# Value products of a slot in two halves by queries, between the score products of the third and fourth head

## The reference

```
h   = layernorm(x) * (1 + ca) + sa                    # ca, sa, ga ... from silu(c) @ wmod, by batch
q, k, v = split(h @ w_qkv)                            # 16 heads of width 8
attn = softmax(q @ k.T / sqrt(128))                   # by head, 512 x 512
x   = x + ga * (concat(attn @ v) @ w_out)
h   = layernorm(x) * (1 + cb) + sb
x   = x + gb * moe(h)                                 # 8 experts of width 176, the best 2 of each token
```

## Time and profile before

| | us |
|---|---|
| median of 3 runs | 652.09 |
| lowest, highest | 651.35, 652.54 |
| the profiled execution's own time | 652.5 |
| its span, first to last instruction | 650.7 |

### The profile page before, as it was taken

How to read it: one execution, slowest core, us unless ns; L and a number is a source line. 1 busy time by engine, 2 the same in 40 slices (tenths; PEclk the granted TensorE clock), 3 DMA queues, 4 the chain that set the end, 5 groups by cost and what they waited for, 6 DMA issues and landing times.

```text
span 650.7 us, 10486 instructions
## 1 busy us (share of the span) xinstructions
PE 600.9 (92%) x3349; PEld 277.9 (43%) x3349; DVE 540.3 (83%) x1025; ACT 433.7 (67%) x823; POOL 300.0 (46%) x426
## 2 busy tenths in 40 slices
PE   4299999999999999999999999897999999999995
PEld 3112222332332322332332322235777777777773
DVE  3698898998998998998998998528788888888884
ACT  1206888788788888888888878774655555555552
POOL 4434205325315315415415212536576776776763
PEclk9757999999999999999999999899899999999998
DMA  7711803402503404404404401263245445444401
GB/s 187 177 65 37 240 3 76 157 19 69 165 19 91 143 20 93 139 21 100 133 19 101 142 9 48 67 191 99 97 133 149 135 136 152 135 136 148 136 24 33
DMA packets 49094, 65.77 MB, mean 101 GB/s; under 512 B 9544, under 2 KB 30544, under 8 KB 49040
## 3 DMA queue, kind: packets, MB, share of 16 engines
q1 hardware_dynamic: 46416, 64.32, 34.3%
q10 hardware_dynamic: 2624, 0.79, 0.6%
HBM read 47.26 MB, written 17.83 MB: 100 GB/s over the span
## 4 chain that ended last, share of the span: by engine, by line
PE 51%; DVE 19%; POOL 15%; issue 6%; ACT 5%; DMA 1%; SPq 1%; POOLq 0%; DVEq 0%; ACTq 0%
PE o_acc L1199 18%; PE s_row L1172 15%; POOL hid_lo L611 11%; DVE negmax L859 8%; DVE probs L1061 8%; PE s_col L1185 7%; ACT hid_hi L795 3%; POOL h_lo L617 2%; PE misc L1137 1%; PE misc L1153 1%; PE misc L1123 1%; PE misc L1120 1%; DVE probs L1051 1%; ACT probs L655 1%; SPq L295 1%
## 5 line engine op out<-in xcount | busy, mean ns | idle before, releaser
L859 DVE TENSOR_REDUCE negmax<-s_row 128x1 f32<-128x512 f32 x512 | 321.3, 682 | 36.9 <-PE s_row L1172 36.1
L655 ACT ACTIVATE probs<-s_col 128x512 f32<-128x512 f32 x512 | 273.3, 599 | 70.7 <-PE s_col L1185 68.5
L1172 PE MATMUL s_row<-k_stack,q_stack 64*128 64x512 bf16 x512 | 140.0, 402 | 21.8 <-DMA k_stack<-k_scr 11.2
L611 POOL TENSOR_TENSOR hid_lo<-probs,hid_hi 128x512 fp32r<-128x512 f32 x87 | 128.5, 1493 | 62.5 <-ACT hid_hi L795 62.5
L1199 PE MATMUL o_acc<-probs,v_aug 128*32 128x512 f32 x1024 | 137.2, 608 | 0.0
L1185 PE MATMUL s_col<-q_stack,k_stack 64*128 64x512 bf16 x512 | 127.5, 381 | 3.2 <-ACT probs L655 2.9
L795 ACT ACTIVATE hid_hi<-probs 128x512 fp32r<-128x512 f32 x88 | 55.6, 632 | 85.3 <-DVE probs L1061 85.3
L1172 PEld LDWEIGHTS s_row<-k_stack,q_stack 64*128 64x128 bf16 x512 | 35.3, 93 | 174.4 <-DVE negmax L859 131.9
L498 POOL CAST negmax_parts<-negmax 128x16 bf16<-128x16 f32 x32 | 6.3, 197 | 154.1 <-DVE negmax L859 154.1
L1061 DVE TENSOR_TENSOR probs<-probs,q_stack 128x512 f32<-128x512 f32 x56 | 61.9, 1106 | 15.4 <-POOL hid_lo L611 14.2
L1051 DVE TENSOR_TENSOR probs<-probs,s_col 128x512 f32<-128x512 f32 x88 | 59.6, 677 | 2.2 <-ACT probs L815 2.1
(11 more groups left out here) (144 smaller groups left out, 697.6 us busy)
## 6 DMA issues: line engine op xcount, KB each, us to landing
q_scr<-q_parts SPq DMA_DIRECT2D x48, 128.0 KB, 2.4
k_scr<-k_parts SPq DMA_DIRECT2D x48, 128.0 KB, 2.4
q_stack<-q_scr SPq DMA_DIRECT2D x8, 768.0 KB, 6.4
k_stack<-k_scr SPq DMA_DIRECT2D x8, 768.0 KB, 8.2
q_stack<-combT_scr SPq DMA_DIRECT2D x24, 256.0 KB, 3.5
k_stack<-combT_scr SPq DMA_DIRECT2D x16, 224.0 KB, 3.0
q_stack<-combT_scr SPq DMA_DIRECT2D x16, 192.0 KB, 2.8
q_stack<-combT_scr SPq DMA_DIRECT2D x16, 160.0 KB, 2.6
```

What stands on the lines that cost most here:

```text
L611: nc.gpsimd.tensor_tensor(hid_lo[k % HIDDEN][:], weighed[(par + k) % 2], hid_hi[k % HIDDEN][:], ALU.subtract).then_inc(s["hid_split"], 1)
L655: nc.scalar.activation(probs[t % 2][:, j, :], s_col[score_bank("col", u)][:], ACT.Exp, scale=INV_SCALE).then_inc(s["exp_done"], 1)
L859: nc.vector.tensor_reduce(negmax[n % 2][:, j, qc:qc + 1], s_row[score_bank("row", u)][:], AX.X, ALU.max, negate=True).then_inc(s["row_max" ...
L1172: nc.tensor.matmul(s_row[score_bank("row", u)][:], q_stack[par][at:at + KS, head // 2, P * qc:P * (qc + 1)], k_stack[par][at:at + KS, head ...
```

## The change

The change splits the value products of a slot into two halves by queries. Part 0 (queries 0 to 255) is issued right after the column scores of head 2, part 1 (queries 256 to 511) where all stood before. Part 0 takes the wait for the exponentials, and part 1 raises `pv_done`. In the four slots whose products open or close a sum in `o_acc` (0, 7, 8 and 15), part 0 is empty and part 1 makes them whole, as before; as slot t makes the products of slot t - 1, these are made in slots 1, 8, 9 and 0 of the loop. The other twelve slots of a batch (2 to 7 and 10 to 15 of the loop) are split.

```diff
-            def weigh(b, par, t):
+            def weigh(b, par, t, part):
                 n, kc = t // CH, t % CH
-                pe.wait_ge(s["exp_done"], UNITS * b + G * (t + 1))
                 m, i = n // SHARE, n % SHARE
                 first_of, last_of = i == 0 and kc == 0, i == SHARE - 1 and kc == CH - 1
+                whole = first_of or last_of
+                if whole and part == 0:
+                    return
+                if whole or part == 0:
+                    pe.wait_ge(s["exp_done"], UNITS * b + G * (t + 1))
                 if first_of and not (isinstance(b, int) and b == 0 and m == 0):
                     pe.wait_ge(s["o_saved"], NO * b + m)
                 values = v_aug[par][:].rearrange("p k h w -> p k (h w)")
+                half = N // 2
+                lo, hi = (0, N) if whole else (half * part, half * (part + 1))
                 for j in range(G):
                     at = VW * (G * n + j) + ROOM * (SHARE - 1 - i)
-                    last = nc.tensor.matmul(o_acc[VW * j:VW * (j + 1), :], values[:, kc, at:at + VW],
-                                            probs[t % 2][:, j, :], start=first_of, stop=last_of)
-                last.then_inc(s["pv_done"], 1)
+                    last = nc.tensor.matmul(o_acc[VW * j:VW * (j + 1), lo:hi], values[:, kc, at:at + VW],
+                                            probs[t % 2][:, j, lo:hi], start=first_of, stop=last_of)
+                if part == 1:
+                    last.then_inc(s["pv_done"], 1)
...
                 for t in range(SLOTS):
+                    def values(part):
+                        if t > 0:
+                            weigh(b, par, t - 1, part)
+                        elif not first:
+                            weigh(b - 1, 1 - par, SLOTS - 1, part)
...
                         for j in range(2 * half, 2 * half + 2):
                             scores(j)
                             col_scores(b, par, t, j)
+                            if j == 2:
+                                values(0)
                         turn((t, half))
-                    if t > 0:
-                        weigh(b, par, t - 1)
-                    elif not first:
-                        weigh(b - 1, 1 - par, SLOTS - 1)
+                    values(1)
                     turn((t, 2))
```

More of the change, by code:

```diff
@@ L1323, in block_body @@
                     if first and k == 0:
-                        weigh(B - 1, 1, SLOTS - 1)
+                        weigh(B - 1, 1, SLOTS - 1, 0)
+                        weigh(B - 1, 1, SLOTS - 1, 1)
                     if first:
```

## The result

The changed kernel takes 679.26 us (median of 4 runs, 676.8 to 689.97) where the kernel before took 652.32 us (4 runs). The ratio is 1.040, with an interval of 1.036 to 1.044: slower. The profiled execution took 677.85 us with a span of 676.0 us, 25.3 us more than the span before.

The account below looks back on a forecast made before the run. PE was taken to set most of a batch, a loop with DVE the slots without a task. Batches 1 to 6 +25.3 us, batch 0 +0.5, batch 7 +1.3: +27.1, forecast 679.2 us, range 666 to 690.

Parts of the forecast that it names:

- step 1: On PE, separating heads 2 and 3 turns 0.53 us into 0.53 + 0.53: +0.53 us wherever the pair ran beside itself.
- step 2: On PE, half of the value products takes 0.57 us, two halves 1.14, so +0.14 us.
- step 3: The 8 weight loads and 8 matmuls more per split slot on PE cost nothing.
- rival C: PE's instruction issue becomes the bound, about 717 us; weaker form, halves of 0.70 us, 696 us; together 15%.
- Rival A: On PE, changes of shape cost nothing extra and heads 2 and 3 overlap with the half between: 647 us, 5%.
- Rival B: Halves cost 0.50 us each, part of the broken pair hides behind waits in slots 4, 5, 14: about 666 us, 17%.
- Rival D: The halves are merged or the order on PE is not kept: 652 us, 1%.
- step 4: The wait for the exponentials moves in front of head 3's scores, but has passed by then: zero cost.
- step 5: In slots without a task, DVE's wait goes: 2.64 us in place of 2.70, set by PE.

## Why the prediction was right

**The broken pair (step 1)** was the number on which the forecast turned, and it held: a lone head takes 0.53 to 0.54 us between two shapes, in any of the three places where runs put it, and where pairs do not exist the split slot costs 0.25 us instead of 0.66.

**The half (step 2)** was put at 0.57 us and took 0.57. That the 0.14 us in it belong to the change of shape is now shown and not argued: two halves in a row take 1.00 us. The rule of the Trainium skill that changing the tiling mode drains the TensorE (TensorEngine Tiling (Array Packing), Key Properties) agrees with these runs: 0.14 us more for halves apart, nothing for halves in a row. The estimate from the fixed part of an isolated matmul (TensorE: Matmul & The Clock Gate, Single matmul latency), 0.33 us for two changes, was too high; the trace has 0.25.

**The instructions (step 3)** cost nothing, as the run with both halves at the end shows. That takes the strong form of rival C away, and the lone 0.57 its weak form. Rival A, no cost for changes of shape, fails on the 0.25 us and on the lone head's 0.54. Rival B wanted halves of 0.50 us and fails on the 0.57; of the slots in which it would hide a part, 4 and 5 cost what was forecast, and only slot 14 cost less. Rival D fails on the 1792 matmuls.

**The moved wait (step 4)** costs nothing that shows: in PE's list of waits no value product waits for ACT, in either trace.

**The gain in plain slots (step 5)** is there at its size, 2.64 us. That DVE's wait can be taken out of these slots is shown by the version with part 0 between the pairs in them alone. How much of the 0.06 us a batch keeps is less sure: with part 0 in the given place, and only there, the whole kernel cannot be told from before.

By slots, forecast and measured from one start to the next: slot 2 3.79 and 3.80; slots 3 and 4 3.32 and 3.33; 5 3.49 and 3.51; 6 3.82 and 3.83; 7 2.64 and 2.64; 10 3.32 and 3.34; 11 3.72 and 3.73; 12 2.81 and 2.81; 13 2.64 and 2.64; 15 3.32 and 3.28. Three sizes were off.

- Slot 14 had 0.25 us for a wait of PE for DVE. It is 3.33 us with no such wait; the row scores of head 1 start together with those of head 0 at 249.43. This is 1.5 us over six batches, and more than all of the difference between 25.3 and 24.2 us; against it the unsplit slots 8 and 9 took 6.24 us in place of 6.17. I had also taken one middle batch for all six; batches 1 and 6 took 48.39 us before and not 48.10.
- Batch 0 was +0.77 instead of +0.5.
- Batch 7 was +0.73 instead of +1.3. Here the clock took part. These stretches lie at the same place of both traces (x1T, the value products behind it and the router; the second is 1 us longer), before and after, with the granted clock in the third column from the end:

```profile
418.00:423.00 5.00, 4.07 (x20) 1.35 (x19) 1.61 (x2) 2.30 (x5) 2.03 (x2) 0.66 0.23 69
```

```profile
444.00:450.00 6.00, 5.07 (x51) 2.33 (x43) 1.99 (x4) 3.97 (x9) 3.42 (x3) 1.00 0.34 109
```

Before, the value products of slot 10 ran at half clock (1.91 us for what takes 1.06), after they did not. PE waited 0.93 us for POOL just ahead of them in both traces, so that pause alone does not decide it. The version with both halves at the end had a granted clock of 1.00 in all of batch 7 and took 43.91 us there:

```profile
391.63:435.54 43.91, 38.25 (x350) 14.84 (x347) 25.82 (x64) 36.38 (x70) 18.35 (x26) 1.00 0.34 96
```

Against it the changed kernel is 1.96 us longer, more than the 1.3 that I had said.

The sum of the profiled executions is thus 25.3 us against my 27.1. The median, 679.26 against 679.2, agrees better than the steps do, and that is chance: it counts the execution of 689.97 us, and without it the median is 677.85.

## What to carry to other kernels

Before something is put between two matmuls, look whether they run beside each other on different rows: two lines of the timeline that start together, with a time no longer than one alone, are one piece of work, and cutting it costs a whole second piece. A finer interleaving pays each change of shape on PE (0.10 to 0.14 us here), so do it only in those slots where PE has a pause, and put the cut at a place where a pair ends. Against some 652.5 us before, part 0 between the pairs took 648.2 us in slots with a pause alone and 655.9 us in all twelve; behind head 2, it took 651.9 us in slots with a pause alone and 679.3 us in all twelve. Where two engines are both above 90% busy, a wait moved from one to the other is not free merely because the slot is bound by the other: follow both through the next slots.

## What the runs showed of the hardware that I had not expected

With all scores on rows 0 to 63, PE's granted clock stayed at 0.50 (1.2 GHz) for the whole attention stage in both traces of the kernel before, with PE counted busy for 340.00 of 340.00 us between 100 and 440 us; a third execution had the same mean clock (0.607 to 0.609 in all three). The changed kernel with the same rows, which differs by the cut and the order of the value products, had 1.00 (2.4 GHz) in its middle batches, in the one execution that there is, and so had both kernels with pairs in their traces. Both start their first scores at 0.50 (30 to 60 us); the one stays there, the other is at 1.00 from 100 to 440 us.

It is not a matter of these rows alone. Of the 44 executions of the kernel before that were timed beside the versions, one took 907.76 us at a mean granted clock of 0.559, and one of ten with both halves at the end took 716.66 us at 0.755. There is no trace of these two, and no run here shows what decides between the two clocks. A kernel can thus be caught at half clock with PE never idle in the profile: its row of the granted clock shows it, the busy share does not.
